# Layer 1's cross-attention of a two-layer Flamingo block: unnormalised probabilities, low halves and context turned by DMA

## The reference

```python
Q  = (X @ Wq.T + bq).reshape(b, lq, 16, 64)            # X: layer norm of x, 56 rows a batch
KV = (encoder_out @ Wkv.T + bkv).reshape(b, lk, 16, 128)
K, V = KV[..., :64], KV[..., 64:]
scores  = einsum('bqhd,bkhd->bhqk', Q, K) / 8
weights = softmax(scores, axis=-1)                       # over the 1500 context rows
attn = einsum('bhqk,bkhd->bqhd', weights, V).reshape(b, lq, h * d)
out  = attn @ Wo.T + bo
```

## Time and profile before

| | us |
|---|---|
| median of three runs | 1364.36 (1363.73 to 1365.16) |
| profiled execution | 1367.69 |
| its span, first to last instruction | 1365.9 |
| TensorE busy | 1222.0 (89%) |
| VectorE busy | 1024.3 (75%) |
| ScalarE busy | 769.0 (56%) |
| GpSimd busy | 395.2 (29%) |
| DMA, mean over the span | 55 GB/s |

### The profile page before, as it was taken

The page is one execution under the profiler, slowest core; times in us unless marked ns, Lnnn a source line. Parts: engine busy times, 40 slices in busy tenths (PEclk is TensorE's granted clock), DMA queues, the critical chain, the costliest instruction groups (busy, mean ns, idle before and its releaser), DMA issues.

```text
span 1365.9 us, 27816 instructions
## 1 busy us (share of the span) xinstructions
PE 1222.0 (89%) x10406; PEld 762.5 (56%) x10408; DVE 1024.3 (75%) x1663; ACT 769.0 (56%) x1013; POOL 395.2 (29%) x248
## 2 busy tenths in 40 slices
PE   0869899999999998788799999999999999999974
PEld 0335566566566566334456666666566666666642
DVE  6656666666666646877788888888888888888877
ACT  0525455555555555455666666666666666666642
POOL 6347666666676414331000000000000000000000
PEclk9979999999999996999999999999999999999996
DMA  5223344344244410010001110011110011110000
GB/s 153 75 78 81 85 108 114 80 113 114 78 109 114 103 60 1 0 46 1 14 32 46 46 46 24 21 45 45 45 45 21 26 43 45 45 45 23 1 0 14
DMA packets 29718, 74.66 MB, mean 55 GB/s; under 512 B 6385, under 2 KB 14961, under 8 KB 29665
## 3 DMA queue, kind: packets, MB, share of 16 engines
q1 hardware_dynamic: 23408, 70.78, 17.9%
q10 hardware_dynamic: 6256, 3.16, 0.9%
HBM read 42.30 MB, written 0.46 MB: 31 GB/s over the span
## 4 chain that ended last, share of the span: by engine, by line
PE 69%; DVE 13%; issue 8%; ACT 6%; ACTq 3%; DVEq 0%; POOL 0%
PE bank L827 13%; PE bank L809 13%; PE bank L769 8%; PE bank L685 7%; PE bank L709 5%; PE bank L713 5%; PE bank L726 4%; DVE bank_max L1498 3%; ACTq L417 2%; DVE region L1642 2%; DVE e_row L1459 2%; PE bank L850 2%; ACT region L1142 2%; PE bank L798 2%; PE bank L1054 2%
## 5 line engine op out<-in xcount | busy, mean ns | idle before, releaser
L1459 DVE CUSTOM_DVE_ANT_0 e_row<-bank,region 112x1500 f32<-112x1500 f32 x128 | 220.1, 1719 | 127.3 <-PE bank L685 126.0
L1177 ACT CAST region<-bank 125x768 f16<-125x768 f32 x224 | 178.7, 798 | 207.7 <-PE bank L769 207.7
L1142 ACT ACTIVATE region<-bank 125x896 f32<-125x896 f32 x192 | 176.0, 917 | 204.8 <-PE bank L713 204.8
L809 PE MATMUL bank<-region 128*128 128x500 f16 x1008 | 234.9, 379 | 14.6 <-ACT e_row L1168 13.1
L1517 DVE TENSOR_TENSOR region<-bank,region 125x768 f16<-125x768 f32 x224 | 209.6, 954 | 26.8 <-ACT region L1177 26.8
L1498 DVE TENSOR_REDUCE bank_max<-bank 128x1 f32<-128x500 f32 x336 | 208.9, 671 | 10.7 <-PE bank L809 10.7
L515 POOL TENSOR_TENSOR region<-c_in,region 125x1536 f16<-125x1536 f32 x16 | 49.6, 3102 | 563.3 <-ACT region L1192 563.3
L769 PEld LDWEIGHTS bank<-ident,e_row 128*125 128x125 f32 x1344 | 176.9, 189 | 31.3 <-DVE region L1517 5.5
L769 PE MATMUL bank<-ident,e_row 128*125 128x128 f32 x1344 | 180.8, 275 | 3.2 <-DVE region L1517 2.6
L1168 ACT ACTIVATE e_row<-bank,neg_max 128x1500 f32<-128x1500 f32 x112 | 169.7, 1515 | 20.2 <-DVE neg_max L1502 19.9
L809 PEld LDWEIGHTS bank<-region 128*128 (+1 forms) x1008 | 93.3, 98 | 115.4 <-issue 11.3
(11 more groups left out here) (213 smaller groups left out, 1473.2 us busy)
## 6 DMA issues: line engine op xcount, KB each, us to landing
c_in<-in_ctx SPq DMA_DIRECT2D x32, 750.0 KB
region<-region SPq DMA_DIRECT2D x64, 192.0 KB, 2.8
region<-in_mask_Bx1xSxS_if SPq DMA_DIRECT2D x32, 328.1 KB
region<-region SPq DMA_DIRECT2D x64, 96.0 KB, 2.6
region<-region SPq DMA_DIRECT2D x8, 750.0 KB
g_w<-region SPq DMA_DIRECT2D x8, 750.0 KB
g_w<-in_L_ffn_rt_gate ACTq DMA_DIRECT2D x1, 1024.0 KB, 10.0
u_w<-in_L_ffn_rt_up ACTq DMA_DIRECT2D x1, 1024.0 KB, 17.3
```

The lines of the kernel that those rows point to most:

```text
L809: last = pe.matmul(bank[:, k, 0:4 * KP], q1[:, ql, b, 128 * t:128 * (t + 1)], c_t1[par][:, cl, 4 * k:4 * k + 4, 0:KP], start=(ql == 0 and ...
L1142: act.activation(p0[:, 2 * i:2 * i + 2, :], ring0("s", h, i)[0:KP, :, 0:HALF_ROWS], ACT.Exp, scale=SCALE0)\
L1177: act.copy(p_high1[grp][:, UC * u:UC * (u + 1), 128 * at:128 * (at + 1)], pair_chunks(unit_no(1, par, ("turn", t, u)), 128)).then_inc(sem( ...
L1459: dve.tensor_tensor_reduce(out=masked.rearrange("p (a k) -> p a k", a=3), in0=bank[0:R0, 0:3, 0:4 * KP], in1=mask_bias[par][:].rearrange(" ...
```

## The change

In layer 1's attention:
- The exponential is shifted so that its largest value is 2^14 (`LIFT` is added to the negated maximum), and the row is not multiplied by the inverse of its sum any more. The maximum is one reduction over three banks. Scores go to banks 0 to 2 and 3 to 5 in turn.
- GpSimd casts the row to float16 (high half) and VectorE subtracts that from the row (low half), both in SBUF before any turn, into `halves1` (two buffers).
- TensorE turns the high half only, in float16, six blocks at a time into one bank (6), and ScalarE copies them out. The low half is turned by a DMA transpose of 128 x 1536 elements from SP.
- The inverse sums of a group are written by DMA to a DRAM scratch and read back spread over all partitions; `dve_scale1` multiplies the products' result by them when it writes `u1`. ScalarE's copy of it is gone.
- The split context is turned by a DMA transpose (for the first batch by TensorE as before).
- The context of batch b + 2 is loaded at batch b.
- A tile's turn and copies stand one tile later than before, the products are spread anew, and the projection is moved to tile 6.
- Some semaphores of other stages are merged; the order of their instructions stays.

The core of the diff (all in the functions of the five engines):

```diff
-    PSCALE = 2.0 ** 14
+    LIFT = 14.0 * math.log(2.0)
...
+        def sync_turn1(sp, b, par, t):
+            grp = 0 if t < GROUPS1[1][0] else 1
+            first = GROUPS1[grp][0]
+            if t == first:
+                wait_apart(sp, "sp", (sem("pv_done1"), 4 * (b - 1) + 2 * grp + 2))
+            wait_apart(sp, "sp", (sem("low_done1"), b * T1 + t + 1))
+            sp.dma_start_transpose(p1[grp][:, 1, :, 128 * (t - first):128 * (t - first + 1)],
+                                   halves1[(t + par) % 2][:, 1].rearrange("p c k -> p (c k)"))\
+                .then_inc(turned1(b, par, t)[0], 16)
+
+        def sync_inverse_out1(sp, b, par, grp):
+            a, z = GROUPS1[grp]
+            wait_apart(sp, "sp", (sem("inv_done1"), b * T1 + z))
+            sp.dma_start(inverse_rows[par, 128 * a:128 * z].rearrange("(t p) -> p t", p=128), row_inv[:, par, a:z],
+                         allow_slow_non_contiguous=True).then_inc(sem("inverse_out1"), 16)
+
+        def sync_inverse_back1(sp, b, par, grp):
+            a, z = GROUPS1[grp]
+            wait_apart(sp, "sp", (sem("inverse_out1"), (2 * b + grp + 1) * 16))
+            wait_apart(sp, "sp", (sem("u_scaled1"), 2 * (b - 1) + grp + 1))
+            sp.dma_start(x_norm_t[:, 128 * a:128 * z],
+                         inverse_rows[par, 128 * a:128 * z].unsqueeze(0).broadcast_to((128, 128 * (z - a))))\
+                .then_inc(sem("inverse1"), 16)
+
+        def sync_turn_context1(sp, b, par):
+            wait_apart(sp, "sp", (sem("split_done1"), b + 1))
+            wait_apart(sp, "sp", (sem("scores1"), (b - 1) * T1))
+            sp.dma_start_transpose(c_t1[par].rearrange("p n c k -> p (n c) k"), c_split1.rearrange("p n c e -> p (n c e)"))\
+                .then_inc(sem("c_turned1"), 16)
...
             def layer1(b, par, first, last):
-                if not last:
-                    sync_load_context(sp, 1, b + 1, 1 - par)
-                    sync_keep(sp, b + 1, 1 - par)
+                if not (isinstance(b, int) and b + 2 >= B):
+                    sync_load_context(sp, 1, b + 2, par)
+                for t in range(T1):
+                    sync_turn1(sp, b, par, t)
+                    if t == 1 and not first:
+                        sync_inverse_back1(sp, b - 1, 1 - par, 1)
+                    if t == 5:
+                        sync_inverse_back1(sp, b, par, 0)
+                    if t in (3, T1 - 1):
+                        sync_inverse_out1(sp, b, par, t // 4)
+                    if t == 2 and not last:
+                        sync_turn_context1(sp, b + 1, 1 - par)
+                    if t == GROUPS1[1][0] and not last:
+                        sync_keep(sp, b + 1, 1 - par)
...
+        def pool_high1(pool, b, par, t):
+            wait_apart(pool, "pool", (sem("exp_done1"), b * T1 + t + 1), (sem("turned_high1"), 2 * (b * T1 + t - 1)))
+            pool.tensor_copy(halves1[(t + par) % 2][:, 0, :, 0:KP], e_row[(t + par) % 2][:].rearrange("p (c k) -> p c k", c=KC))\
+                .then_inc(sem("high_done1"), 1)
...
+            def layer1(b, par, first, last):
+                for t in range(T1):
+                    pool_high1(pool, b, par, t)
+                    if t == 2 and not last:
+                        pool_context1(pool, b + 1, 1 - par)
...
+        def pe_turn1(pe, b, par, t, u, after_proj=False):
+            if u == 0:
+                pe.wait_ge(sem("high_done1"), b * T1 + t + 1)
+            wait(pe, sem("high_copied1"), 2 * (b * T1 + t) + u)
+            if after_proj:
+                pe.wait_ge(sem("block_done1"), b)
...
+            for c in range(UC):
+                last = pe.transpose(turned_half1()[:, 128 * c:128 * (c + 1)], halves1[(t + par) % 2][:, 0, UC * u + c, :],
+                                    ident16[:])
+            last.then_inc(sem("turned_high1"), 1)
...
+                    turn = (b, par, t - 1) if t > 0 else (b - 1, 1 - par, T1 - 1)
+                    proj = t == T1 - 1 and par == 0 and not first
+                    if t >= 5:
+                        product = (b, par, 0, 3 * (t - 5), 3 * (t - 4))
+                    elif t < 2:
+                        product = (b - 1, 1 - par, 0, 3 * (t + 2), 3 * (t + 3))
+                    else:
+                        product = (b - 1, 1 - par, 1, 4 * (t - 2), 4 * (t - 1))
+                    middle = product[4] if t == 1 else product[3] + 2
+                    if proj:
+                        pe.wait_ge(sem("high_copied1"), 2 * (b * T1 + t - 1))
+                        pe_proj1(pe, b)
+                    elif has_turn:
+                        pe_turn1(pe, *turn, 0)
+                    if has_product:
+                        pe_pv1(pe, *product[:4], middle)
+                    if has_turn:
+                        pe_turn1(pe, *turn, 0 if proj else 1, proj)
+                    if has_product and middle < product[4]:
+                        pe_pv1(pe, *product[:3], middle, product[4])
+                    if proj:
+                        pe_turn1(pe, *turn, 1)
...
         def act_exp1(act, b, par, t):
             act.wait_ge(sem("max_done1"), b * T1 + t + 1)
+            wait(act, sem("low_done1"), b * T1 + t - 1)
...
+            dve.wait_ge(sem("scores1"), b * T1 + t + 1)
+            dve.tensor_reduce(neg_max[:, t:t + 1], score_banks1(par, t), AX.XY, ALU.max, negate=True)\
+                .then_inc(sem("raw_max1"), 1)
+            dve.wait_ge(sem("raw_max1"), b * T1 + t + 1)
+            dve.tensor_tensor(neg_shift[:, t:t + 1], neg_max[:, t:t + 1], lift[:], ALU.add).then_inc(sem("max_done1"), 1)
...
+        def dve_scale1(dve, b, par, grp):
+            a, z = GROUPS1[grp]
+            dve.wait_ge(sem("pv_done1"), b * 4 + 2 * grp + 2)
+            dve.wait_ge(sem("inverse1"), (b * 2 + grp + 1) * 16)
+            dve.tensor_tensor(u1[:, par, 128 * a:128 * z], bank[:, U_BANK, 0:128 * (z - a)], x_norm_t[:, 128 * a:128 * z],
+                              ALU.mult).then_inc(sem("u_scaled1"), 1)
+
+        def dve_low1(dve, b, par, t):
+            dve.wait_ge(sem("high_done1"), b * T1 + t + 1)
+            if not (isinstance(b, int) and b == 0 and t < 2):
+                ready, count = turned1(b, par, t)
+                dve.wait_ge(ready, count - 16)
+            half = halves1[(t + par) % 2]
+            dve.tensor_tensor(half[:, 1, :, 0:KP], e_row[(t + par) % 2][:].rearrange("p (c k) -> p c k", c=KC),
+                              half[:, 0, :, 0:KP], ALU.subtract).then_inc(sem("low_done1"), 1)
...
+                    if t in (2, 5) and not first:
+                        dve_scale1(dve, b - 1, 1 - par, 0 if t == 2 else 1)
+                    if not (last and t == T1 - 1):
+                        dve_max1(dve, *nxt)
+                    dve_low1(dve, b, par, t)
+                    dve_inv1(dve, b, par, t)
```

More of the change, by code:

```diff
@@ L653, in _ @@
             pool_rstd(pool, 3, 2 * TT + 4, (4, TT))
-            batches(pool, lambda b, par, first, last: None if last else pool_context1(pool, b + 1, 1 - par))
+            def layer1(b, par, first, last):
[3 more added lines that the diff above has]
+                        pool_context1(pool, b + 1, 1 - par)
+            batches(pool, layer1)
             pool_rstd(pool, 4, 3 * TT, (0, EARLY))
@@ L758, in pe_prep0 @@
             last.then_inc(sem("ct_turned0"), 1)
-        def pe_turn(pe, layer, b, par, t, parts=(0, 1)):
-            if 0 in parts:
-                pe.wait_ge(sem("norm_done1"), b * T1 + t + 1)
-            for u in parts:
-                wait_pair(pe, layer, b, par, ("turn", t, u))
-                n = unit_no(layer, par, ("turn", t, u))
-                for c in range(UC):
-                    k = UC * u + c
-                    last = pe.transpose(pair(n)[0:KP, c // 4, 128 * (c % 4):128 * (c % 4 + 1)],
-                                        e_row[(t + par) % 2][:, KP * k:KP * (k + 1)], ident[:])
-                last.then_inc(sem(f"turned{layer}"), 1)
@@ L773, in pe_prep @@
-        def pe_prep(pe, layer, b, par, halves):
-            for n in halves:
-                if isinstance(b, int) and b == 0:
-                    if n == 0:
-                        wait(pe, sem("const"), 3)
-                else:
-                    wait_pair(pe, layer, b - 1, 1 - par, ("prep", n, 0))
-                pe.wait_ge(sem("split_done1" if n else "high1"), b + 1)
-                no = unit_no(layer, 1 - par, ("prep", n, 0)) if not (isinstance(b, int) and b == 0) else \
-                    n
+        def pe_prep(pe):
+            for n in range(2):
+                pe.wait_ge(sem("split_done1" if n else "high1"), 1)
@@ L1171, in act_high1 @@
         def act_high1(act, b, par, t, u):
-            grp = 0 if t < 4 else 1
+            grp = 0 if t < GROUPS1[1][0] else 1
             at = t - GROUPS1[grp][0]
-            act.wait_ge(sem("turned1"), (b * T1 + t) * 2 + u + 1)
-            if at == 0 and u == 0:
-                wait(act, sem("pv_done1"), (b - 1) * 2 + grp + 1)
```

(6 more changed lines are left out.)

309 lines of the change are left out of this document (129 added, 180 removed).

## The result

The changed kernel takes 1473.94 us (median of 4, 1470.17 to 1479.15) beside 1364.41 for the kernel before (1363.73 to 1365.16): a ratio of 1.0805, 95% interval 1.0772 to 1.0839. It is 110 us slower. I had forecast 1274, and none of the rivals, at 1256, 1303 to 1340, 1366 and 1697, meets the time.

A forecast was written before the change was run, and what follows sets the result against it. TensorE was taken to bound layer 1 at 41.17 us a batch; 33.6 + 0.4 + 0.3 + 1.1 = 35.4 us saves 92 us over 16, less 2 in the tail: 1274 us, range 1243 to 1330.

The forecast's parts named there:

- the rivals: 1256: no port loss, 0.14; 1303 to 1340: DMA turns late, 0.17; 1366: nothing won, 0.03; 1697: DMA turns set pace, 0.14.
- the inverse sums go out as 896 pieces of 4 bytes (1.7 us at 31 ns): Layer 1, DMA engines: writing the sums takes 1.7 us a batch, part of 35.0 us of DMA work.
- rival C: Layer 1: DMA turns set the pace once one takes over 3.7 us; at 6.0, 62.0 us a batch, 1697 us; chance 0.14.
- ten us or more: Layer 1: time between sending or asking back each group's inverse sums and the tile that wants them.
- rival B: Layer 1: DMA turns land in 7.5 us instead of 5.1 (1303), or need 3.5 us of the engines (1340); chance 0.17.
- TensorE's sum: Layer 1: TensorE's work falls from 39.4 to 33.6 us a batch, the 1.7 us of stalls gone; period 35.4.
- The port: Layer 1, tile 2: VectorE's two-input SBUF subtraction waits for GpSimd's context subtraction, 1.1 us a batch, between 0 and 2.5.
- over 3 in tile 2: Expected sign in layer 1: VectorE's subtraction takes near 1.7 us alone and over 3 us in tile 2.
- The DMA turns: Layer 1: each tile's turn takes 3.0 us of the 16 engines and lands in 5.1; nine make 27 us a batch.
- It just fits: Layer 1: 35.0 us of DMA work a batch fits within a period of 35.4 us.
- Context two ahead: Layer 1: loading the context two batches ahead gains nothing, since the load was never waited for.
- the tail: End of layer 1: last scores to the last block grows from 18.5 to 19.3 us; 2 us taken as cost.

The follow-up runs named there:

- inverse_16B: Changed kernel with inverse sums sent to DRAM in SBUF order, one 16- or 12-byte piece a partition, VectorE reading them with a stride: 1294.14 us, ratio 0.9489.
- two_parts: 16-byte-piece kernel with constant shift, plus GpSimd's context subtraction halved over tiles 2 and 3 and the context's turn after tile 3's: 1308.05 us, ratio 0.9584.

## Why the prediction was wrong, point by point

- **The step that failed** is the term "the inverse sums go out as 896 pieces of 4 bytes (1.7 us at 31 ns)". I priced the pieces by their own time, and there I was even too high: 9 ns each, 0.5 us. Their price is what they do to the packets behind them: some 11 us at about a quarter of the rate behind one write, at some 60% behind the other. So twice a batch the next DMA turn lands late. Taking the writes away, spacing them or joining them gives 1286 to 1294 us; leaving only them gives 1475. I looked for the danger in the volume of the turns (rival C) and made the trip's slack ("ten us or more") the only other question about the sums. That slack was there: VectorE's scaling never waited for them.
- **Where the lateness lands** was half right, and the sign given for rival B (VectorE idle before its subtraction, put down to a DMA) is what the trace shows. B named tile 0's turn, wanted by tile 2's subtraction, with a room of about 5.7 us; the landing was 14. The other wait of each batch, tile 6's subtraction for tile 4's turn, is in no rival. What B also lacked is the cause, and the second part of the price: after a pause of 7 us TensorE works at the 1.2 GHz level, 3.1 us a batch that no sum of mine had.
- **TensorE's sum** held. Clean tiles take 4.53 to 4.64 us (forecast 4.60), the batch without the inverse trip 36.4, in the repaired kernel (inverse_16B) 400 / (689 / 63) = 36.6, forecast 35.4. The missing 1.2 x 16 = 19 us is nearly all that separates 1274 from 1294. So the sum without the trip was sound; that it came within 20 us of the repaired kernel does not make the forecast right, since the change as made had the trip in it.
- **The port** costs 1.75 us where nothing else is late, instead of 1.1, and 0.6 a batch in the time; and it does so by another instruction than I named: not the subtraction but the shift, 0.16 us of work on two columns in SBUF, which takes 2.00 until GpSimd's 3.10 us subtraction is over, as in the earlier trace rows. The Trainium skill, "SBUF — State Buffer" (section SBUF: two separate sides), says that the pair of ports is locked for a whole instruction when VectorE has two inputs in SBUF, whichever comes first; the trace agrees (here GpSimd came first; in two_parts, at 901.58, VectorE did, and GpSimd's half of 1.64 us took 3.11). With the constant in place of the second column the shift takes 0.15, but the subtraction behind it has two inputs again and took 3.4 us in 6 of some 11 batches: the "over 3 in tile 2" of the forecast.
- **The DMA turns** were priced at 3.0 us of the 16 engines. In the repaired kernel a 256-byte row took 18 ns in the median and 26 in the mean, so 1536 x 18 / 16 = 1.7 us by the one and 2.5 by the other. They land in 3.9 to 4.0 us instead of 5.1. "It just fits" was too cautious for that kernel: its DMA engines are busy 0.81 of 36.6 us, 29.6 instead of 35.0. The Trainium skill, "DMA: Bandwidth & Descriptors" (section Latency and other measured facts), gives the 261 GB/s that I had set beside it at 1.5 us; the median row comes near that, the mean does not. The 1309 ns a block of the Trainium skill, "VectorE: DVE Perf Modes" (section The three transpose paths), is not paid once per block: twelve blocks land in 3.9 us.
- **Context two ahead: "nothing"** holds in the sum, since the load is waited for neither before nor after. But as a statement on this part of the change it hides 88 us: without it, the load would be issued 1.3 us ahead of its cast instead of 31, because SP's program now follows the tiles.
- **The small prices** held: the maximum 1.71 us in the mean (forecast 1.70), the subtraction 1.72 (1.72), float16 turns six in 0.34 (0.056 each), the shift 0.16. So did the tail: from the last scores' end to the last part 20.8 us in the changed kernel as in the repaired one, against 18.5; I had taken 2 more.

What stays open is why adjacent 4-byte writes hold the queues. No run tells whether it is the memory (several writes into one small stretch of it) or the DMA engines that write it, nor where between 4 and 64 bytes of spacing it ends. It is not the context's reading from DRAM alone, since the copy inside SBUF is slowed too. The joined pieces of 12 or 16 bytes also lie side by side and cost 8 us at most; whether that is owed to their size or to there being 128 of them instead of 512 or 384, no run separates.

## What to carry to other kernels

Price a small transfer by what queues behind it, too: here 384 writes of 4 bytes side by side in DRAM slowed a busy set of queues to a quarter for eleven microseconds, while the waits blamed the innocent transfer behind them. Give each piece 64 bytes of its own, or keep the DRAM layout that of SBUF so that the pieces are joined. And when a wait names a DMA, read what SP issued just ahead of it before cutting that DMA down.

## What the runs showed of the hardware

- 896 writes of 4 bytes a batch: adjacent 1475 us, 64 bytes apart 1288, 512 apart 1290, joined to 12 or 16 bytes 1294. The Trainium skill, "DMA: Bandwidth & Descriptors" (section Why small descriptors are slow (HBM only)), knows a fixed cost for each small piece; that cost would be the same in the first three, so it isn't this.
- SP's issue of a DMA turn of 12 blocks takes 1.45 us, of 1 block 1.1, of the context's 24 blocks 3.8, of a plain copy with the same rows 0.6; behind the 4-byte writes it took up to 9.95, and SP issued nothing else meanwhile.
- GpSimd's product of 128 x 1500 numbers with a column takes 4.07 us, its cast 1.44. VectorE's multiply-and-subtract with a column takes 1.78 us, its subtraction 1.72; beside GpSimd's context subtraction of 3.10 us the first took 4.5 to 4.6, and the mean of all 59 is 2.16.
